# Reciprocal roots of the narrow and the cross attention's norms as one power on GpSimd

## The reference, cut to what matters

```python
def _layernorm(x, eps=1e-05): return (x - mean(x)) / sqrt(var(x) + eps)
def _rms(x, g):  return x * rsqrt(mean(x*x) + EPS) * g        # narrow attention: 16 heads of 16 channels
    q = _rms(h, g_q) @ Wq + bq;  k, v = _rms(h, g_kv) @ Wkv + bkv
    scores = _rms(q, g_head) @ _rms(k, g_head).T * d**-0.5;  softmax;  @ v;  @ Wo + bo
def _rmsnorm(x, w): return x * rsqrt(mean(x*x) + 1e-6) * w    # cross attention: 16 heads of 128 channels
x = x + narrow_attention(_layernorm(x))
x = x + cross_attention(_layernorm(x), ctx, mask)
```

## Time and profile before

| | |
|---|---|
| runs shown | 1831.98, 1838.97, 1837.02 us; median 1837.02 |
| the profiled execution | 1832.67 us, of which the span in the profile is 1830.9 us |
| PE busy | 1622.8 us, 89% of the span |
| DVE busy | 1132.0 us, 62% |
| ACT busy | 971.9 us, 53% |
| POOL busy | 537.7 us, 29% |
| mean granted PE clock | 0.943 of full speed |

### The profile page before, as it was taken

The page is one execution under the profiler, slowest core; times in us unless marked ns, Lnnn a source line. Parts: engine busy times, 40 slices in busy tenths (PEclk is TensorE's granted clock), DMA queues, the critical chain, the costliest instruction groups (busy, mean ns, idle before and its releaser), DMA issues. The chain is left out here.

```text
span 1830.9 us, 25838 instructions
## 1 busy us (share of the span) xinstructions
PE 1622.8 (89%) x8598; PEld 1303.0 (71%) x8598; DVE 1132.0 (62%) x2496; ACT 971.9 (53%) x2789; POOL 537.7 (29%) x447
## 2 busy tenths in 40 slices
PE   6999989889988768899999859999889999999866
PEld 5888877778777656667777647777667887888634
DVE  4654685577577676354443464643447778767878
ACT  4645545445454553223323545677747666676756
POOL 2242332733442271311002365445022122211000
PEclk9999999999999989999999957988789999999989
DMA  7153333422543162143433311000030111000001
GB/s 271 47 178 110 124 139 126 170 98 98 185 149 108 43 166 64 58 127 108 130 106 125 116 46 30 27 4 24 1 135 20 42 40 33 13 1 1 1 1 47
DMA packets 87512, 151.50 MB, mean 83 GB/s; under 512 B 9941, under 2 KB 45397, under 8 KB 87381
## 3 DMA queue, kind: packets, MB, share of 16 engines
q1 hardware_dynamic: 81236, 133.07, 22.2%
q0 software_dynamic: 6144, 16.79, 2.9%
HBM read 90.84 MB, written 58.98 MB: 82 GB/s over the span
## 5 line engine op out<-in xcount | busy, mean ns | idle before, releaser
L790 PE MATMUL bank<-self_attention 128*128 128x256 f32 x512 | 127.7, 394 | 26.4 <-DVE residual L1680 18.1
L2598 ACT ACTIVATE cross_attention_heads<-cross_attention_heads,small 128x128 f32<-128x128 f32 x256 | 99.6, 390 | 89.2 <-DVE small L2033 89.2
L2342 ACT ACTIVATE self_attention<-self_attention,small 128x128 f32<-128x128 f32 x256 | 100.0, 392 | 83.7 <-DVE small L1666 83.2
L1126 PE MATMUL bank<-cross_attention,cross_attention_heads 128*128 128x256 f32 x512 | 125.0, 387 | 15.3 <-DVE residual L2047 10.0
L790 PEld LDWEIGHTS bank<-self_attention 128*128 128x128 f32 x512 | 98.2, 195 | 46.5 <-DVE residual L1680 24.4
L595 PE MATMUL bank<-x_channel_major,qkv_weights_split 128*128 128x512 f32 x256 | 117.8, 460 | 7.3 <-DVE qkv_weights_split L1698 2.9
L1126 PEld LDWEIGHTS bank<-cross_attention,cross_attention_heads 128*128 128x128 f32 x512 | 95.9, 192 | 38.8 <-DVE residual L2047 18.9
L2510 ACT ACTIVATE narrow_late<-bank,small 128x128 f32<-128x128 f32 x256 | 91.0, 376 | 58.2 <-DVE small L1904 57.5
L2702 POOL CAST qkv_weights_split<-self_attention 128x1024 fp32r<-128x1024 f32 x45 | 50.6, 1125 | 223.0 <-DMA self_attention<-in_wqkv 198.5
L2704 POOL TENSOR_TENSOR qkv_weights_split<-self_attention,qkv_weights_split 128x1024 fp32r<-128x1024 f32 x45 | 109.5, 2433 | 3.6
L888 PE MATMUL bank<-experts,tiles 128*128 x316 | 108.0, 465 | 0.4 <-DVE tiles L1782 0.4
(11 more groups left out here) (398 smaller groups left out, 4725.1 us busy)
## 6 DMA issues: line engine op xcount, KB each, us to landing
picked_inputs<-self_attention SPq DMA_DIRECT2D x64, 512.0 KB
self_attention<-in_wqkv SPq DMA_DIRECT2D x48, 512.0 KB
experts_far<-picked_inputs SPq DMA_DIRECT2D x79, 128.0 KB, 2.1
picked_outputs<-tiles SPq DMA_DIRECT2D x79, 128.0 KB, 1.7
self_attention<-in_wo SPq DMA_DIRECT2D x16, 512.0 KB
experts<-in_moe SPq DMA_DIRECT2D x4, 1408.0 KB
self_attention<-in_bv SPq DMA_DIRECT2D x16, 256.0 KB, 5.1
context_values<-context_out SPq DMA_DIRECT2D x16, 256.0 KB
```

The lines of the kernel that those rows point to most:

```text
L790: m = T.matmul(bank[7][:, 0:D], ZT_a[n % 2][:, h, :], wo_a[p % 2][:, h, :], start=h == 0, stop=h == HG - 1)
L1126: m = T.matmul(bank[7][:, 0:D], ZT_x[n % 2][:, h, :], x_wo[hg % 2][:, h, :], start=h == 0, stop=h == HG - 1)
L2342: m = S.activation(P_a[u][:, h, :], P_a[u][:, h, :], ACT.Exp, bias=negmax_a[u][:, h:h + 1], accum_out=sums_a[u][:, h:h + 1])
L2598: m = S.activation(P_x[u][:, h, :], P_x[u][:, h, :], ACT.Exp, bias=negmax_x[u][:, h:h + 1], accum_out=sums_x[u][:, h:h + 1])
```

## The change

GpSimd makes the reciprocal root in one go: a multiply-add gives variance times scale plus epsilon, and one two-input instruction raises it to a power of -0.5, which is read from a broadcast column `minus_half`. This replaces ACT's `Sqrt` and DVE's reciprocal for the norms `second` (narrow attention) and `cross` (all four groups of each, `FIRST_POWER` to `LAST_POWER`), and for the narrow attention's head norms. The norms of other stages keep the two steps. POOL's new instructions stand at fixed places of its order: for group 0 of the narrow attention before the squares and, for the head norms, after `gather(7)`; in the loop one iteration after the moments and one after `ROOT`, in place of a wait on DVE; for the last cross group after the first squared queries.

```diff
+FIRST_POWER, LAST_POWER = NORM["second", 0], NORM["cross", NG - 1]
 # VectorE
-                V.reciprocal(rstd[:, s, :], sd[:, s, :]).then_inc(dve.own, dve.tick())
+                if not FIRST_POWER <= i <= LAST_POWER:
+                    V.reciprocal(rstd[:, s, :], sd[:, s, :]).then_inc(dve.own, dve.tick())
...
-                    V.reciprocal(rstd[:, s, :], sd[:, s, :]).then_inc(dve.own, dve.tick())
-                    dve.settle()
-            narrow_inverse(0)
-                if n - 1 in ROOT:
-                    narrow_inverse(ROOT[n - 1])
 # ScalarE
-            deviations(NORM["second", 0], eps_both, 1.0 + RMS_EPS)
-            narrow_root(0)
-                if n in MOMENTS and MOMENTS[n][1]:
-                    deviations(NORM["second", MOMENTS[n][0]], eps_both, 1.0 + RMS_EPS)
-                if n in ROOT:
-                    narrow_root(ROOT[n])
-                if n - 1 in CROSS_MOMENTS:
-                    deviations(NORM["cross", CROSS_MOMENTS[n - 1]], eps_ln, 1.0)
 # GpSimd
+            def inverse_deviations(i, eps, scale):
+                s = i % 2
+                pool.wait_ge(ln_stats, i + 1)
+                G.tensor_scalar(rstd[:, s, :], mv[:, s, :, 1], scale, eps, ALU.mult, ALU.add).then_inc(pool.own, pool.tick())
+                pool.settle()
+                G.tensor_tensor(rstd[:, s, :], rstd[:, s, :], minus_half[:, 0:1].broadcast_to([P, GB]), ALU.pow).then_inc(ln_sd, 1)
+
+            def narrow_inverse(g):
+                every = qss[:, g % 2].rearrange("p b c -> p (b c)")
+                pool.wait_ge(n_summed, GB * g + GB)
+                G.tensor_scalar(every, every, 1.0 / DS, RMS_EPS, ALU.mult, ALU.add).then_inc(pool.own, pool.tick())
+                pool.settle()
+                G.tensor_tensor(every, every, minus_half[:, 0:1].broadcast_to([P, GB * 32]), ALU.pow).then_inc(n_inverse, 1)
+                pool.wait_ge(n_inverse, g + 1)
...
             gather(7)
+            narrow_inverse(0)
             head_norm(0)
...
+                if n - 1 in MOMENTS and MOMENTS[n - 1][1]:
+                    inverse_deviations(NORM["second", MOMENTS[n - 1][0]], RMS_EPS * LN_EPS, 1.0 + RMS_EPS)
+                if n - 1 in CROSS_MOMENTS:
+                    inverse_deviations(NORM["cross", CROSS_MOMENTS[n - 1]], LN_EPS, 1.0)
...
                 if n - 1 in ROOT:
+                    narrow_inverse(ROOT[n - 1])
                     for b in range(GB):
                         head_norm(GB * ROOT[n - 1] + b)
...
+            x_square(0)
+            inverse_deviations(NORM["cross", NG - 1], LN_EPS, 1.0)
```

More of the change, by code:

```diff
@@ L253, in build @@
         shared_gate = sm.take(B)
+        minus_half = sm.take(2)
         rest = sm.take(GB * CW).rearrange("p (b c) -> p b c", b=GB)
@@ L1895, in narrow_sums @@
                 V.tensor_reduce(qss[:, g % 2, b, :], n_sq.rearrange("p (c d) -> p c d", d=DS), AX.X, ALU.add).then_inc(n_summed, 1)
-            def narrow_inverse(g):
-                dve.wait_ge(n_root, g + 1)
-                V.reciprocal(qss[:, g % 2], qss[:, g % 2]).then_inc(n_inverse, 1)
             def narrow_scores(n):
@@ L2217, in second_norm @@
                     deviations(NORM[stage, g], eps_both, 1.0 + RMS_EPS)
-                else:
-                    deviations(NORM[stage, g], eps_ln, 1.0)
                 yield from pause(5 if apart else 3)
@@ L2488, in turn_keys @@
                              scale=kscale[:, 0:1]).then_inc(c_kT.sem, 1)
-            def narrow_root(g):
-                act.wait_ge(n_summed, GB * g + GB)
-                S.activation(qss[:, g % 2], qss[:, g % 2], ACT.Sqrt, bias=eps_rms[:, 0:1], scale=1.0 / DS).then_inc(n_root, 1)
             def narrow_heads(bb):
@@ L2834, in gpsimd_program @@
                 pool.wait_ge(stored_out[s], 16 * ((NTILE - 1 - s) // NYS + 1))
+            G.memset(minus_half[:, 0:1], -0.5).then_inc(pool.own, pool.tick())
+            pool.settle()
             for bb in range(7):
                 gather(bb)
+            def inverse_deviations(i, eps, scale):
[8 more added lines that the diff above has]
+                G.tensor_scalar(every, every, 1.0 / DS, RMS_EPS, ALU.mult, ALU.add).then_inc(pool.own, pool.tick())
+                pool.settle()
+                G.tensor_tensor(every, every, minus_half[:, 0:1].broadcast_to([P, GB * 32]), ALU.pow).then_inc(n_inverse, 1)
+                pool.wait_ge(n_inverse, g + 1)
             def square(bb):
@@ L2872, in gpsimd_program @@
             pool.wait_ge(got_narrow, 64)
+            inverse_deviations(NORM["second", 0], RMS_EPS * LN_EPS, 1.0 + RMS_EPS)
             for b in range(GB):
@@ L2904, in gpsimd_program @@
             pool.wait_ge(n_added, B)
-            for f in range(LEAD):
+            x_square(0)
+            inverse_deviations(NORM["cross", NG - 1], LN_EPS, 1.0)
+            for f in range(1, LEAD):
                 x_square(f)
```

## The result

The changed kernel takes 1900.14 us (median of 6 runs, 1894.68 to 1905.26) against 1834.5 us for the kernel before, run beside it: a ratio of 1.0357 with a 95% interval of 1.0326 to 1.0389. It is slower by 65.6 us, where 12 us less had been forecast, and outside the range of 1813 to 1852. The profiled execution took 1897.37 us, with a span of 1895.6. In the experiments a difference from before is the ratio less one, times the median of the kernel before that was run beside. The ratios leave out three runs (one of 12, two of 10) that took over 1.5% longer than the fastest of their kernel.

A forecast was written before the change was run, and what follows sets the result against it. PE was taken to bound most of the kernel through its waits and clock, POOL alone the opening. Terms +3.8 - 0.5 - 8.0 - 3.0 - 0.9 + 1.0 + 0.2 - 4.5 = -11.9 us from 1837.02 gave 1825, range 1813 to 1852.

The forecast's parts named there:

- P: Price of one 128x128 power on POOL: taken as 3.3 us, with bounds of 0.5 and 12.3.
- the prediction's own formula: Whole kernel: -11.9 + (P - 3.3) + 3(P - 3.77) us, with opening and three loop places paying for P.
- The rival of the dear power: Opening and three loop places: a 128x128 power over 8.9 us makes the kernel slower, 1860 us; chance 0.23.
- Opening: Group 0's head norms: the power stands between POOL's gathers and head norms with nothing hiding it, +3.8 us.
- The 0.5 of group 0's norm: Opening: PE's wait of 0.47 us for normalised tiles behind ACT's root goes, -0.5 us.
- Head norms in the loop: Three places: power free up to P = 3.77 us, excess paid at each; PE's wait for ACT's late copy goes, -0.9.
- Narrow layer norms: Groups 2 and 3 in the loop: PE's waits of 1.49 us behind ACT's table reload go, -3.0 us.
- Cross norms and the clock: Cross norms' stretch: PE's waits go, -8.0 us, and a third of the clock's loss returns, -4.5 (bounds nothing and 13.5).
- Cross group 3: After the loop: multiply-add and power take about as long as ACT's root and DVE's reciprocal, 0.
- DVE beside a busy POOL: Two of three loop places: a combine step under the power is slowed, 0.5 us each, +1.0.
- The start-up: Rival at group 0's norm: the first power is dear once, sum -8.6 us, no change; chance 0.07.
- Table loads: ACT: 17 fewer loads of 1.283 us, 21.8 us of ACT, but only what PE waits for counts.

The follow-up runs named there:

- the 16 and 32 columns: Layer norms' powers kept, opening's head norms as before, loop's head norm power over only 16 or 32 of 128 columns: ratios 0.9901 and 0.9983 against before.
- the kernel of prices: All computation left out; single POOL, then DVE instructions, each waiting for the one before: power 1.02 us at 4 columns, 41.12 at 256.

## Why the prediction was wrong

The step that failed is the price of the power, P: "I take a power as two functions of that kind", 3.3 us, with 12.3 above. It measured 20.76. Both numbers were scaled from DVE's reciprocal, and the bound of "four times as dear a function" rested on no row of POOL computing one. With P = 20.76 the prediction's own formula gives -11.9 + 17.5 + 3 x 17.0 = +56.6, against 65.6 measured; the size of P alone takes the sum from faster to slower. Of the 9.0 us left over, 5.9 are PE's waits in the loop beyond the formula (below); the rest isn't split. The rival of the dear power named the mechanism, its places and the point from which it decides (8.9 us), with a chance of 0.23; its time of 1860 was too low for the same reason.

- **Opening.** "Nothing hides it" was right: 21.2 us by the formula with the measured P, and 21.2 by PE's wait. The 0.5 of group 0's norm was there as well: DVE's wait of 2.24 us is down to 0.37, and PE's of 0.47 is gone.
- **Head norms in the loop.** No wait up to a slack, 1:1 beyond: right for PE's waits, as the 16 and 32 columns show; the loop of the profile with 32 columns is 8.7 us longer, for 5.8 of waits. The slack is not one number: 3.77 us was read from group 1 of before, and in the kernel of the layer norms' powers the three places leave 1.55, 4.30 and 3.93. PE's waits in the changed kernel sum to 20.15 + 17.01 + 19.72 = 56.9 where the formula gives 51.0.
- **Narrow layer norms.** 3.0 us were taken from waits of 1.49, and nothing for the clock. With these powers alone PE's idle time in the two stretches falls by 2.0 us and the loop by 8.4, most of it busy time at a higher clock; the whole measured 5.3 less. In the changed kernel PE's clock behind the new waits takes more than that back: in group 2's stretch 329 matmuls are busy for 64.05 us at 0.70, against 330 for 56.68 at 0.87.
- **Cross norms and the clock.** The places were right and the clock mis-sized. PE's idle time in their stretch falls from 8.7 to 2.5 us (6.2 against 8.0 forecast for the waits), and its busy time for the same matmuls from 41.55 to 30.50, because the clock goes from 0.73 to 1.00: 11.1 us where 4.5 had been taken, inside the bound of 13.5. The argument that PE would soon wait for ACT failed, since ACT's work there falls from 36.1 to 28.6 us with its table loads.
- **Cross group 3.** It was put at 0; PE's wait before its transposes grows from 1.06 to 1.83 us.
- **DVE beside a busy POOL.** The 1.0 us was for nothing: beside the power four combine steps take 2.05 us, as four took 2.04 in the kernel before while POOL computed nothing (at 1030.46). One by itself takes 0.48, and 0.96 beside a product.
- **The start-up.** The first power in the program takes 1.01 us in the kernel of prices, and the same size later 1.02. In the changed kernel DVE goes on 1.08 us after POOL's first power started. The Trainium skill (GPSIMD Engine Reference, 2.1 "Instruction dispatch") gives about 6 us for the first call of a freshly loaded routine; no run here shows that for the power.
- **Table loads.** 17 fewer, as counted, each of 1.283 us before and after. The Trainium skill (ScalarE: Activation LUTs, "What ACT_TABLE_LOAD costs") adds a drain of about 1.38 us to each switch; by that figure, an estimate, the five loop places would have given 14 us more. The traces don't agree: the root starts 0.02 us behind its load, and PE's idle time at these places fell by 6.2 + 2.0 us, less than the 8.0 + 3.0 forecast without a drain.

The version to keep is one with no power for the head norms: the layer norms' powers alone took 0.9923 and 0.9904 of before in two timings, the cross norms' alone 0.9871 and 0.9904. Which of these two is faster isn't shown.

## What to carry to other kernels

Another engine's rows give no upper bound for an operation that no row prices: here 12.3 us was the bound and 20.76 the price. When the sum changes sign inside what the operation might cost, measure the operation first, by itself and at two widths; two such numbers would have decided this case. Then cost each place alone: the same power was worth a gain at 4 columns, where it hid under a wait, and a loss at 128, where it stood ahead of everything. Idle time on the engine that takes the work is a budget to be added up from its rows, place by place; beyond it the next engine waits for every us. And compare profiles stretch by stretch: the same code ahead of the loop ended up to 7.2 us apart on one chip, more than several of the effects here.

## What the runs showed of the hardware

POOL's power takes 0.159 us a column plus 0.38 us (1.02 us at 4 columns, 41.12 at 256), with 32 or 128 partitions and with the exponents -0.5, 0.5 and 2 (20.70 to 20.73 us at 128 columns); a product of 128x128 takes 0.45. DVE's combine steps aren't slowed beside it (2.05 us for four, against 2.04 while POOL computes nothing), as they are beside a product (0.96 for one, against 0.48). And PE's clock was worth more than the waits that went: in the cross norms' stretch the granted clock rose from 0.73 to 1.00, which took 11.1 us from PE's busy time, while its idle time fell by 6.2.
